# Cross attention's query fold moved into self attention's turns, and its softmax sums placed later

## The reference, cut to what matters

```
q   = ln(fp8_linear(h, wq))            k = ln(fp8_linear(h, wk))       # self attention
qx  = ln(fp8_linear(h, wqx))           kx = ln(cond @ w_kv_x[:G*D].T)  # cross attention
out = softmax(q  k^T  / sqrt(128)) v          self
      softmax(qx kx^T / sqrt(128)) vx         cross, vx = cond @ w_kv_x[G*D:].T
```

## Time and profile before

| what | value |
|---|---|
| median of 3 runs | 2561.54 us |
| profiled execution / its span | 2560.54 / 2558.5 us |
| TensorE matmul busy | 2341.7 us, 92% |
| VectorE busy | 2019.6 us, 79% |
| ScalarE busy | 1088.3 us, 43% |
| GpSimd busy | 919.4 us, 36% |
| first to last `L1350` start (self attention) | 797.8 to 1083.4 us |
| first `L1784` to last `L1807` start (cross attention) | 1117.1 to 2251.4 us |

### The profile page before, as it was taken

How to read it: one execution, slowest core, us unless ns; L and a number is a source line. 1 busy time by engine, 2 the same in 40 slices (tenths; PEclk the granted TensorE clock), 3 DMA queues, 4 the chain that set the end, 5 groups by cost and what they waited for, 6 DMA issues and landing times. The chain is left out here.

```text
span 2558.5 us, 38343 instructions
## 1 busy us (share of the span) xinstructions
PE 2341.7 (92%) x12603; PEld 2045.3 (80%) x12603; DVE 2019.6 (79%) x3952; ACT 1088.3 (43%) x1849; POOL 919.4 (36%) x640
## 2 busy tenths in 40 slices
PE   7999999999984788859999999999999999986797
PEld 6777777779983666658888888988888888976797
DVE  8999987877757887848888888888888888871487
ACT  1000001108855666614544554455545454554332
POOL 5455100200012344424545544555455444570000
PEclk9999999999996888879999999999999999997899
DMA  9667623517624010042222212222222112106211
GB/s 389 263 266 274 240 99 145 191 66 255 220 98 144 37 44 36 29 135 77 84 74 79 69 46 80 83 80 69 74 83 71 63 57 83 61 4 162 56 55 39
DMA packets 143384, 286.66 MB, mean 112 GB/s; under 512 B 26033, under 2 KB 114178, under 8 KB 139202
## 3 DMA queue, kind: packets, MB, share of 16 engines
q1 hardware_dynamic: 137266, 265.40, 30.0%
q0 software_dynamic: 6032, 20.20, 2.1%
HBM read 203.91 MB, written 81.66 MB: 112 GB/s over the span
## 5 line engine op out<-in xcount | busy, mean ns | idle before, releaser
L1697 POOL TENSOR_TENSOR s_acc<-s_acc,s_sx 125x896 f32<-125x896 f32 x128 | 275.8, 2154 | 261.3 <-DVE s_mxh L1941 114.6
L572 DVE BATCH_NORM_STATS2 s_st<-ps 125x6 f32<-125x128 f32 x1536 | 318.7, 280 | 55.6 <-PE ps L444 49.1
L1896 DVE TENSOR_TENSOR s_sx<-ps,keep_krs 125x896 f32<-125x896 f32 x192 | 208.9, 1088 | 167.3 <-PE ps L1807 164.1
L1761 ACT ACTIVATE s_sx<-s_sx 125x896 f32<-125x896 f32 x192 | 183.2, 954 | 352.8 <-DVE s_sx L1914 352.8
L1858 PE MATMUL ps<-s_p_hi,s_cn_hi 125*128 125x448 f32 x768 | 304.1, 396 | 6.6 <-DVE s_p_lo L1920 6.2
L1920 DVE TENSOR_TENSOR s_p_lo<-s_sx,s_p_hi 125x896 fp32r<-125x896 f32 x192 | 290.7, 1514 | 3.1 <-ACT s_p_hi L1766 3.1
L1807 PE MATMUL ps<-s_qc_hi,s_ct_hi 128*125 128x448 f32 x768 | 288.3, 375 | 1.3 <-DVE s_qc_lo L1879 1.3
L1858 PE MATMUL ps<-s_p_lo,s_cn_hi 125*128 125x448 f32 x768 | 285.1, 371 | 0.0
L1858 PE MATMUL ps<-s_p_hi,s_cn_lo 125*128 125x448 f32 x768 | 285.1, 371 | 0.0
L1807 PE MATMUL ps<-s_qc_lo,s_ct_hi 128*125 128x448 f32 x768 | 282.5, 368 | 0.0
L1807 PE MATMUL ps<-s_qc_hi,s_ct_lo 128*125 128x448 f32 x768 | 282.3, 368 | 0.0
(11 more groups left out here) (378 smaller groups left out, 5646.1 us busy)
## 6 DMA issues: line engine op xcount, KB each, us to landing
l_ahead<-in_ctxt SPq DMA_DIRECT2D x16, 1500.0 KB, 8.6
s_ct_hi<-ct_hi SPq DMA_DIRECT2D x48, 500.0 KB, 4.2
s_ct_lo<-ct_lo SPq DMA_DIRECT2D x48, 500.0 KB, 4.9
s_cn_raw<-in_ctx SPq DMA_DIRECT2D x48, 500.0 KB
l_raw<-in_ctxt SPq DMA_DIRECT2D x15, 1500.0 KB, 10.4
l_raw<-in_w SPq DMA_DIRECT2D x16, 1024.0 KB, 5.4
ct_hi<-l_hi SPq DMA_DIRECT2D x8, 1500.0 KB, 12.1
ct_lo<-l_lo SPq DMA_DIRECT2D x8, 1500.0 KB, 16.3
```

Source lines behind the costliest of these rows:

```text
L572: ins = dve.bn_stats(st[:, G * t + g, :], kx[0:TT, t % NB, g // 4, DH * (g % 4):DH * (g % 4) + DH])
L1697: pool.tensor_tensor(a, a, p[:, PR * w.pt:PR * w.pt + PR, :], ALU.add).then_inc(s["acc_ready"], 1)
L1761: act.activation(p, p, ACT.Exp).then_inc(s["exp_ready"], 1)
L1896: dve.tensor_tensor(by_group(sx[w.h][:, tiles, :]), by_group(sc[st % 2]), krs_b[:, tiles, HG * w.h:HG * w.h + HG].unsqueeze(3).to_broadcas ...
```

## The change

Self attention gets the fold. `spread` now writes a cross query chunk into one of two small buffers (`qxr`, laid over the weight ring, which is idle by then). From slot 8 on, each slot t has two folds of chunk t-8, one per half of the model width (kk 0 and 1), each of two matmuls with 224 columns. The first stands after `turn_heads`, the second after the slot's scores and values. Both write PSUM bank 6, shared with the turned probabilities, and ScalarE copies each out (`take_fold`) into `qcs`, which is twice as large as `qxs` was. SyncE stores `qcs` to `qc` in DRAM.

Cross attention loads the folded queries (twice the bytes, one load per batch) and splits them from SBUF: one ScalarE copy and one VectorE subtraction of 896 columns per unit in place of two each of 448 columns from PSUM. TensorE has no fold. Its values stand ahead of the small work of steps 3 to 5. VectorE's reciprocal of the sums goes to the end of step 3; ScalarE's `rdiag` goes from step 3 to 4 and `rsc` from step 4 to 5; the product `ca` goes from VectorE's step 5 to step 0 of the next unit.

```diff
 # self attention
+        qxr = [w[r][:, 0, 0:QC * PAIR].rearrange("p (h n) -> p h n", h=QC) for r in range(2)]
+        qcs = m.sb("qcs", [P, 2, K2, NH, S])
+        folded = ps[:, 6, 0:QC * PAIR]
+        FOLDS = K2 * NQ
+        FIRST_QX = NK + NQ
+        FOLD_AT = FIRST_QX + 2
...
+                        if not (early(p, 1) and q < 2):
+                            act.wait_ge(s["fold_ready"], FOLDS * p + K2 * (q - 1))
+                        if early(p, 1) and q == 0:
+                            act.wait_ge(s["w_lo_ready"], CHUNKS)
+                        out, wt, bs = qxr[q % 2][:, :, :], qxw[:, 0:1], qxb[:, 0:1]
...
+                def take_fold(p, q, kk):
+                    act.wait_ge(s["fold_ready"], FOLDS * p + K2 * q + kk + 1)
+                    if q == 0 and kk == 0 and not early(p, 1):
+                        act.wait_ge(s["qx_stored"], 32 * p)
+                    act.activation(qcs[:, :, kk, QC * q:QC * q + QC, :].rearrange("p b h s -> p h b s"),
+                                   folded.rearrange("p (h b s) -> p h b s", h=QC, b=2), ACT.Copy).then_inc(s["fold_read"], 1)
...
                             spread(p, t - 1)
+                        if live and t >= FOLD_AT:
+                            take_fold(p, t - FOLD_AT, 0)
                         input_work(SCALED, t, i, par, scale_input)
...
                         at_slot(EXPS, t, p, exp)
+                        if live and t >= FOLD_AT:
+                            take_fold(p, t - FOLD_AT, 1)
...
+                def fold_queries(p, q, kk):
+                    pe.wait_ge(s["tr_read"], NORMED * p + FIRST_QX + q + 1)
+                    if q == 0 and kk == 0 and not early(p, 1):
+                        pe.wait_ge(s["prt_read"], NQ * p)
+                    if not (early(p, 1) and q == 0 and kk == 0):
+                        pe.wait_ge(s["fold_read"], FOLDS * p + K2 * q + kk)
+                    half = QC // HPG
+                    for j in range(half):
+                        mm = pe.matmul(folded[:, HPG * PAIR * j:HPG * PAIR * j + HPG * PAIR], keep.wk[:, half * q + j, kk * P:kk * P + P],
+                                       qxr[q % 2][:, HPG * j:HPG * j + HPG, :], start=True, stop=True)
+                    mm.then_inc(s["fold_ready"], 1)
 # cross attention, ScalarE and VectorE
+                def qc_split(u, h):
+                    act.activation(qc_hi[h][:, :, :], q[:, :, QH * h:QH * h + QH], ACT.Copy).then_inc(s["qc_hi_ready"], 1)
...
+                def qc_split(u, h):
+                    dve.wait_ge(s["qc_hi_ready"], u + 1)
+                    dve.tensor_tensor(qc_lo[h][:, :, :], q[:, :, QH * h:QH * h + QH], qc_hi[h][:, :, :].bitcast(F32), ALU.subtract).then_inc(s["qc_lo_ready"], 1)
...
-                    if w.i in (2, 3) and w.next and w.new:
-                        qc_split(w.u + 1, 1 - w.h, w.i - 2)
+                    if w.i == 2 and w.next and w.new:
+                        qc_split(w.u + 1, 1 - w.h)
 # cross attention, TensorE: the values (if w.has_v) now stand ahead of steps 3 to 5's small work
-                        if w.new and w.next:
-                            pe.wait_ge(s["qc_lo_ready"], K2 * w.u + 2 * K2)
-                    if w.i == 1 and w.new and w.next:
-                        fold_queries(w.u + 1, 1 - w.h, 0)
-                    if w.i == 2 and w.new and w.next:
-                        fold_queries(w.u + 1, 1 - w.h, 1)
```

More of the change, by code:

```diff
@@ L1404, in turn @@
                             turn_heads(p, t - 1)
+                        if not beyond(p) and t >= FOLD_AT:
+                            fold_queries(p, t - FOLD_AT, 0)
                         at_slot(SCORES, t, p, scores)
@@ L1407, in turn @@
                         at_slot(VALUES, t, p, lambda q, a: values(q, a, 1 - par))
+                        if not beyond(p) and t >= FOLD_AT:
+                            fold_queries(p, t - FOLD_AT, 1)
                         if early(p, 1) and t == 4:
@@ L1615, in steps_of @@
             body(B)
+            act(B + 1, 0)
             act(B + 1, 3)
@@ L1776, in _ @@
             def _(pe):
-                def fold_queries(u, h, k):
-                    if h == 0 and k == 0:
-                        pe.wait_ge(s["q_loaded"], 8 * u + 16)
-                    for j in range(HG):
-                        g = HG * h + j
-                        mm = pe.matmul(misc[:, PAIR * j:PAIR * j + PAIR], wk[:, g, k * P:k * P + P], q[:, PAIR * g:PAIR * g + PAIR],
-                                       start=True, stop=True)
-                    mm.then_inc(s["qc_ready"], 1)
-                fold_queries(0, 0, 0)
-                pe.wait_ge(s["qc_lo_ready"], 1)
-                fold_queries(0, 0, 1)
                 def run(b, st):
@@ L1821, in run @@
                         pe.matmul(mb, ones_r[:, :], diag[:, :, :], start=True, stop=True).then_inc(s["mb_ready"], 1)
+                    if w.has_v:
+                        pe.wait_ge(s["lo_ready"], w.v + 1)
+                        if w.vt == 0 and not (static(w.vu) and w.vu < 1):
+                            pe.wait_ge(s["ut_read"], w.vu)
+                        if w.vh == 0 and PR * w.vt % CHT == 0:
+                            vb = b + (st - V_LAG) // STEPS
+                            pe.wait_ge(s["cn_lo_ready"], NCH * vb + PR * w.vt // CHT + 1)
+                        for j in range(PR):
+                            t = PR * w.vt + j
+                            for k in range(K2):
+                                c = 0
+                                for x, pp in ((cn_hi, (p_hi, p_lo)), (cn_lo, (p_hi,))):
+                                    for y in pp:
+                                        mm = pe.matmul(pv[:, k, :], x[:, t, k * P:k * P + P], y[w.vr][:, j, :],
+                                                       start=(t == 0 and c == 0), stop=(t == NT - 1 and c == 2))
+                                        c += 1
+                        mm.then_inc(s["pv_ready"], 1)
                     if w.i == 3 and w.two_back:
@@ L1886, in run @@
                     tiles = slice(PR * w.i, PR * w.i + PR)
-                    if w.i == 3 and w.next and w.new:
-                        qc_split(w.u + 1, 1 - w.h, 1)
                     if w.new:
@@ L1902, in run @@
                         dve.tensor_reduce(m4[:, :], misc[0:PAIR, 0:HG * TT].rearrange("p (g n) -> p g n", g=HG), AX.X, ALU.max).then_inc(s["mt_read"], 1)
-                    if w.i == 2 and w.next and w.new:
-                        qc_split(w.u + 1, 1 - w.h, 0)
-                    if w.i == 3 and w.two_back:
-                        dve.wait_ge(s["sum_ready"], w.u - 1)
-                        if not (static(b) and w.u < 3):
-                            dve.wait_ge(s["rdiag_ready"], w.u - 2)
-                        dve.reciprocal(r4[:, :], sums).then_inc(s["r4_ready"], 1)
+                    if w.i == 3 and w.next and w.new:
+                        qc_split(w.u + 1, 1 - w.h)
                     if w.has_p:
@@ L1946, in run @@
                             dve.tensor_tensor(mx[:, :], mxh[:, 0, :], mxh[:, 1, :], ALU.max).then_inc(s["mx_ready"], 1)
+                    if w.i == 3 and w.two_back:
+                        dve.wait_ge(s["sum_ready"], w.u - 1)
+                        if not (static(b) and w.u < 3):
+                            dve.wait_ge(s["rdiag_ready"], w.u - 2)
+                        dve.reciprocal(r4[:, :], sums).then_inc(s["r4_ready"], 1)
                 steps_of(dve, None, run)
```

92 lines of the change are left out of this document (30 added, 62 removed).

## The result

| | us | runs |
|---|---|---|
| before | 2559.88 (2557.67 to 2563.57) | 4 |
| after | 2540.24 (2536.91 to 2541.83) | 4 |
| after / before | 0.992, interval 0.9903 to 0.9937 | |
| profiled execution after, its span | 2541.07, 2539.0 | 1 |

A forecast was written before the change was run, and what follows sets the result against it. TensorE was taken to bound cross attention (busy 71.5 of 72.7 us), no engine being full in self attention. 2560.5 - 58 (cross attention) + 47 (self attention) = 2549.5, said as 2549 us; range 2526 to 2578.

The forecast's parts named there:

- Self attention, forecast +47: Self attention: folds and their copies lengthen seven turns by 5.7 us each and the last by 7, 47 us in all.
- Rival D: Self attention: if the hole shrinks and TensorE's clock stays at 2.4 GHz, 7 turns give back 14 us: 2535; chance 0.12.
- Cross attention, forecast -55: Cross attention, first to last score: 76 us given up by TensorE, less 21 us that come back through late VectorE work.
- the wait ahead of the sums: Cross attention: TensorE's wait before the sums, for the second low part, goes with its bank conflict, 21 us over all units.
- What comes back: Cross attention: collisions with GpSimd make VectorE late for TensorE, mean 0.7 us per unit, 21 us; bounds 0 and 42.
- The forecast's two waits: Cross attention, units with GpSimd's context low part: 0.3 us before step 4's values, 1.05 before the reciprocals' broadcast, for `rdiag`.
- the other small work only change places: Cross attention: the sums (0.81 us) and other small work on TensorE were taken to move without cost or gain.
- The chain it did follow: Cross attention, steps 2 to 4: GpSimd's context low part delays VectorE's maximum, then the reciprocal and `rdiag`, in 16 of 32 units.
- B: Cross attention: the collisions don't hold TensorE up, so the 21 us stay gained: 2528; chance 0.15.
- E: Cross attention: the late reciprocal bites in both halves, 11 us more than counted: 2560, no change; chance 0.13.
- The bound of 74 us: Cross attention: 31 new VectorE subtractions each blocked by a whole 2.39 us GpSimd instruction, as much as 74 us, less VectorE's slack.
- Behind the last score, forecast -1.5: End of cross attention: sums stand behind the last values, which no longer wait for GpSimd's sum; 1 to 2 us, taken as 1.5.

The follow-up runs named there:

- the third experiment: The changed kernel with GpSimd's low part of the context only 16 of 256 columns wide from the second batch on, the rest left out: 2503.4 us, ratio 0.9772.

## Why the prediction was right, and where its sizes were off

**Self attention, forecast +47, measured +41.5.** The slots were forecast at 3.8 us and are 3.85; slot 11 was forecast at +1.2 and is +1.24. These make 3 x 1.55 + 1.24 = 5.9 us, and yet a turn grows by (285.9 - 252.3) / 7 = 4.8. Most of the missing microsecond is a misreading: the earlier trace rows show a turn of the shorter kind. In the longer ones of the kernel before TensorE waits in the middle of slot 11's projection as well, for an input that GpSimd prepares. Such a row, and that wait between 850 and 1100 us:

```profile
1018.88 0.48 PE L1350 MATMUL ps<-s_w_hi,s_xq 128*112 128x512 f32 x1 [1.53 <-POOL s_xq L1195]
```

```profile
PE ps L1350 <- POOL s_xq L1195: 4.7, 3, 1.6
```

There slot 11's projection starts at 1016.18 and slot 1's at 1022.20, 6.0 us later and not 4.17. After has no such wait in that stretch: the fold stands in the hole. So the longer turns grow by 4.1 to 4.2 us, the shorter ones by 5.8 to 5.9, where 5.7 was forecast; the first grows by 3.6.

Rival D gave nothing, though the clock did rise. The time at 1.2 GHz per turn fell from 10.2 and 13.7 us in turn to 6.8, and the clock of the stretch is 0.92 against 0.86 of the earlier trace rows. But from slot 1's projection to slot 8's, where the slow time lies, it takes the same 23.8 us at every clock, in both kinds of turn before (the first two rows) and in after (the third):

```profile
985.42:1009.18 23.76, 19.56 (x97) 15.27 (x98) 19.17 (x48) 17.59 (x35) 11.94 (x12) 0.78 0.05 19
1022.20:1045.96 23.76, 21.07 (x97) 16.22 (x98) 19.19 (x48) 17.56 (x35) 13.15 (x14) 0.73 0.05 19
```

```profile
1012.53:1036.29 23.76, 18.58 (x97) 14.75 (x98) 19.17 (x48) 17.56 (x35) 11.92 (x12) 0.86 0.23 92
```

TensorE is faster there and waits longer for the others, as the prediction's own argument against D said.

From the load of the queries to the first score are 7.7 us in place of 10.2, so the start gives 2.5 where 2 were forecast, and the last turn, 39.0 + 2.5 - 33.6, costs 8 where 7 were.

**Cross attention, forecast -55 between first and last score, measured -57.6.** Both sides of the sum were larger, and that they came out within 3 us of the forecast is in part luck. Kept without collisions (the third experiment) the gain is 1127.2 - 1038.4 = 89 us, where the prediction had 76. The folds measure 54 of it, as forecast. For the rest the term "the wait ahead of the sums", 21 us, was too small: the order alone gives 32. By the units, it saves 0.5 us in a light one (35.6 to 35.1) and 1.2 in a heavy one (36.4 to 35.2), together some 24 us. The other 8 are four of before's heavy units, 38.0 to 38.6 us long and not 36.4, and in each the clock falls 2 us after such a wait. One of them, by stretch, and TensorE as it begins:

```profile
1301.40:1304.70 3.30, 3.30 (x10) 2.94 (x9) 2.88 (x6) 1.18 (x4) 0.00 (x0) 0.50 0.01 2
```

```profile
1301.19 0.37 PE L1858 MATMUL ps<-s_p_hi,s_cn_lo 125*128 125x448 f32 x1
1301.40 0.54 PE L1858 MATMUL ps<-s_p_hi,s_cn_hi 125*128 125x448 f32 x1
1301.73 0.58 PE L1858 MATMUL ps<-s_p_lo,s_cn_hi 125*128 125x448 f32 x1
```

Matmuls that were 0.205 us apart are 0.33 to 0.37 apart, at 1.2 GHz. At 1.6 to 2.2 us over a usual heavy unit the four cost 8 us together; in three of them some 0.4 us of it is a wait for the low part. Before has 14 waits of 1.0 us ahead of the sums and such a stretch behind four of them. After, with waits of 0.8 us at most, has none between 1206 and 2246 us, the order alone none between 1126 and 2228, and the kernel with `ca` sooner, with waits of 2 us, 13 in 14. That they come from the waits is thus what these traces agree on, not shown: no run changed the clock alone, and ten waits of 1.0 us had none behind them.

What comes back was forecast at 21 us and is 1069.6 - 1038.4 = 31. The forecast's two waits were 0.3 and 1.05 us per heavy unit, 1.35; they measure 0.56 and 0.51 of idle time, and 0.17 of draining for each as in the earlier trace rows, 1.41 together. The step that fell short is that "the other small work only change places": `ca`, now in step 0, stands on VectorE behind a subtraction and the low part, and TensorE's turning of the maxima waits for it, 6.3 / 14 + 0.17 = 0.6 us per heavy unit. The prediction priced the move of `ca` nowhere. The chain it did follow was right to its marks: the maximum of step 2 near 3 us (3.29), the light half free, TensorE late in the other. That settles rivals B and E too: TensorE is held up in every heavy unit, against B, and in no light one, against E. One mark was off in size: the wait for `rdiag` is 0.51 us where about 1 was forecast, and the one ahead of it, for the low part, 0.56 where 0.3 was.

The rule weighed there, SBUF — State Buffer, section "SBUF: two separate sides", in the Trainium skill (the pair of ports is held by one of VectorE and GpSimd for a whole instruction) is borne out by the 3.29 and 3.24 us above, and by the 1.08 us of those with a PSUM input. The bound of 74 us that the prediction worked out for the new subtraction did not come: all 32 take 1.07 to 1.09 us in after. In the heavy unit above GpSimd was waiting then, as the prediction argued.

**Behind the last score, forecast -1.5, measured -4.4.** The order alone gives 6 there, and the old order with the moved fold gives none (77.3). So it is the new order, as forecast, and its gain was counted at a quarter. Which of its parts it is, the values ahead of the last small work or another, no run tells apart.

**What the split of the sum did not say.** The sum priced the change as one thing. Its parts are -36.8 us for the order and +16.9 for moving the fold on top of it. The forecast's own terms already said something of it: the wait and the end were worth 22 us without any fold moved, and the folds' 55 less the collisions' 21 fall short of the 45 paid. What they missed is the size, 37 against 22 and 17 against 11. With the fold in TensorE's stream a unit lasts 35.1 us and VectorE keeps up in both halves. Without it the light unit goes to 33.3 and the heavy one to 35.5. So half of the units return 1.8 us and the other half lose 0.4: 16 x 1.8 - 16 x 0.4 = 22 us, measured 1095.2 - 1069.6 = 25.6, for 39.7 us paid in self attention (365.0 - 325.3). The best of these kernels that leaves nothing out is the one with the order alone, 2523.3 us.

**Open.** Whether an arrangement of VectorE's and GpSimd's instructions exists in which both halves take 33.3 us with the fold moved: it would be worth about as much as the run with the small low parts, 2503. None of the five that were tried came near (the old order, the reciprocal sooner, `ca` too, the queries' subtraction too, the parts spread). Why the old order costs a unit 0.6 us without a wait. And what makes the clock fall in cross attention behind some waits of 1 us and not behind others.

## What to carry to other kernels

Work that is moved away from a full engine is worth only what the next engine lets through: compare its busy share in the shorter period, half by half if the period alternates, and not over the mean. Read one turn of every kind before taking it for all: here every second one had a hole that the rows chosen did not show. When a change has a part that moves work and a part that reorders it, run the reorder alone; here it was worth nearly twice the whole. A removed idle microsecond may be worth more than itself, where the clock falls behind it; and a faster clock is worth nothing in a stretch where TensorE waits for others.

## What was not expected of the hardware

A lead of 0.05 us over GpSimd is enough for VectorE's 125 x 896 instruction to take 1.09 us; 0.48 us behind it, it takes 2.85. Putting 0.54 us of work ahead of it made the kernel 39 us slower, from 2540 to 2579. In the heavy unit shown the one that has waited goes next, so that the two alternate: 1.76, 3.24 and 3.29 us for instructions that take 1.08, 2.39 and 1.08 alone.

TensorE's clock fell to 1.2 GHz for 3.3 us behind waits of no more than about 1 us, four times in 31 units, and behind waits of 2.1 us 13 times in 14. In self attention a clock of 0.73, 0.78 or 0.86 made no difference to a stretch of 23.8 us.
